# A four-layer attention and expert network: the last attention's maxima in four parts, its bodies 0.45 of a unit behind them

## The reference, cut to what matters

```python
def _L3_xattn_ref(x, cond, Wq, bq, Wkv, bkv, Wp, bp):
    q = (x @ Wq + bq).reshape(1, B * N, H, hd)          # 1024 queries, 16 heads of 16
    kv = (cond @ Wkv + bkv).reshape(1, -1, 2, H, hd)    # 1024 keys: all batches attend to all
    q = _fq_sym(q * scale, axis=-1)                     # rounded to 8 bits, one scale per token and head
    k = _fq_sym(k, axis=-1)
    v = _fq_sym(v, axis=2)
    attn = softmax(q @ k.T)
    attn = _fq_unsigned(attn, axis=-1)                  # round(attn / (max / 255)) * (max / 255)
    return (attn @ v).reshape(B, N, C) @ Wp + bp
x = x + tanh(g_xattn[3]) * _L3_xattn_ref(layernorm(x), ctx, ...)
x = x + tanh(g_ffn[3]) * _L3_ffn_ref(layernorm(x), ...)
```

## Time and profile before

| | us |
|---|---|
| median of 3 runs (1188.04 to 1189.3) | 1189.02 |
| the profiled execution's own time | 1187.16 |
| its span, first to last instruction | 1185.4 |
| TensorE busy in the span | 945.1 |
| VectorE busy | 660.6 |
| ScalarE busy | 438.3 |
| GpSimd busy | 383.5 |

### The profile page before, as it was taken

The page is one execution under the profiler, slowest core; times in us unless marked ns, Lnnn a source line. Parts: engine busy times, 40 slices in busy tenths (PEclk is TensorE's granted clock), DMA queues, the critical chain, the costliest instruction groups (busy, mean ns, idle before and its releaser), DMA issues.

```text
span 1185.4 us, 18900 instructions
## 1 busy us (share of the span) xinstructions
PE 945.1 (80%) x6620; PEld 558.2 (47%) x6620; DVE 660.6 (56%) x1574; ACT 438.3 (37%) x722; POOL 383.5 (32%) x515
## 2 busy tenths in 40 slices
PE   3899985798299999777379726999989997199993
PEld 1455544687044456554247612344434444156662
DVE  5678753462679334777623358787887852211111
ACT  1366662111056313443014300466546575021220
POOL 5233204332631003442050061356555565200002
PEclk9999996989589999996589956699999999599997
DMA  6434524684543004542327530101210002700002
GB/s 183 122 102 146 175 82 186 187 291 153 125 113 83 1 1 121 173 95 67 142 102 227 170 95 15 41 2 42 108 42 2 2 3 108 267 21 23 14 14 80
DMA packets 112700, 116.32 MB, mean 98 GB/s; under 512 B 58824, under 2 KB 102408, under 8 KB 109576
## 3 DMA queue, kind: packets, MB, share of 16 engines
q1 hardware_dynamic: 101760, 96.62, 26.5%
q10 hardware_dynamic: 7776, 10.10, 2.6%
q0 software_dynamic: 3072, 8.39, 2.3%
HBM read 88.17 MB, written 30.67 MB: 100 GB/s over the span
## 4 chain that ended last, share of the span: by engine, by line
PE 47%; DVE 14%; DMA 7%; issue 7%; POOL 6%; ACT 2%; SPq 1%; POOLq 0%; ACTq 0%; DVEq 0%
PE psT L1523 7%; PE psT L1223 5%; PE psT L1374 5%; PE psB L1338 4%; DVE mxp L1929 4%; PE psB L1223 4%; PE psO L1418 3%; PE psB L1537 3%; PE psT L1486 2%; PE psB L1588 2%; PE psO L1408 2%; DMA scr_k_high<-sk 1%; PE psO L1406 1%; POOL scr_sorted L2354 1%; PE psB L1564 1%
## 5 line engine op out<-in xcount | busy, mean ns | idle before, releaser
L1929 DVE TENSOR_REDUCE mxp<-psB 128x1 f32<-128x512 f32 x256 | 163.7, 684 | 37.5 <-PE psB L1338 36.7
L1374 PE MATMUL psT<-whole 99*128 99x256 bf16 (+2 forms) x1024 | 153.1, 275 | 10.0 <-issue 9.0
L1933 DVE TENSOR_REDUCE mxp<-psB 128x2 f32<-128x512 f32 x192 | 123.5, 684 | 31.6 <-PE psB L1344 31.2
L1675 ACT ACTIVATE Pt<-psT,ln 128x1024 f32<-128x1024 f32 x96 | 106.7, 1114 | 63.8 <-PE psT L1374 62.7
L1374 PEld LDWEIGHTS psT<-whole 99*128 99x128 bf16 (+2 forms) x1024 | 96.5, 102 | 54.1 <-issue 21.5
L1675 ACT ACTIVATE Pt<-psT 128x1024 f32<-128x1024 f32 x96 | 98.1, 1024 | 58.3 <-PE psT L1374 56.6
L1338 PE MATMUL psB<-whole 96*128 96x512 bf16 x256 | 96.2, 427 | 24.3 <-DMA whole<-scr_q 13.9
L2283 POOL TENSOR_TENSOR rstd<-vare,cst 128x1 f32<-128x1 f32 x64 | 35.8, 562 | 231.3 <-DVE vare L1836 231.0
L1344 PE MATMUL psB<-whole 96*128 96x256 bf16 x384 | 78.0, 306 | 36.0 <-DMA whole<-scr_q 20.3
L1523 PE MATMUL psT<-whole,qf 128*128 x176 | 82.3, 612 | 0.6 <-ACT qf L1729 0.6
L2342 POOL TENSOR_SCALAR nb_t<-Pt 128x1024 f16<-128x1024 f32 x64 | 67.2, 1051 | 39.5 <-ACT Pt L1675 37.4
(11 more groups left out here) (323 smaller groups left out, 1743.8 us busy)
## 6 DMA issues: line engine op xcount, KB each, us to landing
whole<-in_w SPq DMA_DIRECT2D x32, 512.0 KB, 5.2
whole<-in_w SPq DMA_DIRECT2D x5, 3072.0 KB, 10.3
xn<-scr_sorted ACTq DMA_DIRECT2D x42, 128.0 KB, 2.2
scr_q<-sq SPq DMA_DIRECT2D x48, 96.0 KB, 2.2
whole<-scr_q SPq DMA_DIRECT2D x24, 192.0 KB
whole<-scr_k SPq DMA_DIRECT2D x24, 192.0 KB, 3.5
scr_sorted_out<-xn SPq DMA_DIRECT2D x31, 128.0 KB, 2.4
scr_k<-sk SPq DMA_DIRECT2D x32, 96.0 KB, 1.9
```

Source lines behind the costliest of these rows:

```text
L1374: ins = pe.matmul(psT[:, s.n % 2, i * A.T:(i + 1) * A.T], lhsT=k_at[:, h * kw + s.c * P:h * kw + (s.c + 1) * P], rhs=q_at[:, h * A.T:(h + ...
L1675: act.activation(p_slot(A, s.p)[:, 0:4 * A.T], psT[:, s.n % 2, 0:4 * A.T], ACT.Exp, bias=bias, scale=scale).then_inc(T_used[s.n % 2], 1)
L1929: dve.tensor_reduce(mxp[:, s.un.g % 2, at:at + 1], psB[:, s.n % BANKS, :], AX.X, ALU.max).then_inc(bank_used[s.n % BANKS], 1)
L1933: dve.tensor_reduce(mxp[:, s.un.g % 2, at:at + 2], psB[:, s.n % BANKS, :].rearrange("p (h n) -> p h n", h=2), AX.X, ALU.max).then_inc(bank ...
```

## The change

The last attention has four parts in place of two (`parts=4`), so one part is 16 tiles of maxima and serves one group. Its times are set anew: maxima from `u + 1.0` to `u + 2.0`, each part's `negmax` 0.05 behind its end, the body at `u + 1.45`, the end at `u + 3.15`. The front of unit 1 is moved from `1 + t` to `1 + 0.17 + 0.6 t`. And the split of unit 0's queries is made on VectorE, where GpSimd only waits for it. The number of parts is now the unit's (`r.parts`), and the other attentions get new names for the same times: their order stays as it was.

```diff
+FIRST_PARTS = (1, 1, 1, 4)
+SECOND_FRONT = (0.17, 0.6)
...
-                           NC=chunks, has_max=has_max, G=heads // 4, halves=heads * d // P, parts=2 if layer == 3 else 1,
+                           NC=chunks, has_max=has_max, G=heads // 4, halves=heads * d // P, parts=4 if layer == 3 else 1,
...
-    dict(front=0, fronts=[...], rest=[...], store=0.42, packs=0.43, max=0.909, max_end=1.919, neg=1.973, body=1.639, end=3.415, start=0, span=1.008, max_first=1.026)]
+    dict(front=0, fronts=[...], rest=[...], store=0.42, packs=0.43, max=1.0, max_end=2.0, neg=2.05, body=1.45, end=3.15, start=0, span=1.0, max_first=1.0, first_end=2.0, first_body=1.45, first_neg=0.05, max_second=1.0)]
...
+            r.parts = FIRST_PARTS[A.layer] if u == 0 else A.parts
...
-            per = A.H * A.NC * P // 512 // A.parts
-            for part in range(A.parts):
+            per = A.H * A.NC * P // 512 // r.parts
+            for part in range(r.parts):
...
+                if A.layer == 3 and u == 1:
+                    times = [SECOND_FRONT[0] + SECOND_FRONT[1] * t for t in times]
...
-                begin = u + at["max"] if u else at["max_first"]
-                step = (u + at["max_end"] - begin) / A.parts
+                begin = at["max_first"] if u == 0 else 1 + at["max_second"] if u == 1 else u + at["max"]
+                end = at["first_end"] if u == 0 else u + at["max_end"]
+                step = (end - begin) / units[u].parts
+                later_by = at["neg"] - at["max_end"] if u else at["first_neg"]
...
-            streams += [(body(units[u]), u + at["body"], body_end), (finish(units[u]), body_end + at["start"], u + at["end"]),
+            streams += [(body(units[u]), u + at["body"] if u else at["first_body"], body_end), (finish(units[u]), body_end + at["start"], u + at["end"]),
...
-                elif s.kind == "split" and s.kind_of == "q" and s.un.u == 0:
+                elif s.kind == "split" and s.kind_of != "k1" and s.un.u == 0 and s.A.layer in (1, 3) and s.un.g is not None:
...
+                    else:
+                        evacuated(dve, u.m[0])
+                        evacuated(dve, u.m[1])
+                        src = qf[:, u.g % 2, :]
                     dve.wait_ge(parts_q, u.g)
                     dve.wait_ge(q_stored[u.g % 2], 32 * (u.g // 2))
-                    high, middle, low = [sq[:, u.g % 2, i, 0:256] for i in (2, 1, 0)]
-                    link(dve.tensor_copy(high, xn[:, 0, :]))
-                    link(dve.tensor_tensor(tmp[:, 0:256], xn[:, 0, :], high, ALU.subtract))
+                    high, middle, low = [sq[:, u.g % 2, i, 0:w] for i in (2, 1, 0)]
+                    link(dve.tensor_copy(high, src))
+                    link(dve.tensor_tensor(tmp[:, 0:w], src, high, ALU.subtract))
...
-                    if s.kind_of == "q" and u.u == 0:
+                    if u.u == 0 and u.g is not None and A.layer in (1, 3):
                         pool.wait_ge(parts_q, u.g + 1)
```

More of the change, by code:

```diff
@@ L69, in __init__ @@
         self.b0 = b0
-        self.k_packed = self.k_packed_before = None
+        self.k_packed = self.k_packed_before = self.parts = None
 P = 128
@@ L145 @@
 TIMES = [
-    dict(front=0.339, store=0.638, packs=0.793, max=1.019, max_end=1.817, neg=1.926, body=2.312, end=3.927, start=0.17, span=1.026, max_first=1.418),
-    dict(front=0.315, store=0.667, packs=1.608, max=1.871, max_end=2.713, neg=2.846, body=3.334, end=5.364, start=0, span=0.958, max_first=2.13),
-    dict(front=0.368, fronts=[-0.15, 0.1, 0.278, 0.262, 0.45], store=0.58, packs=0.684, body=1.604, end=3.227, start=0.084, span=1.053),
-    dict(front=0, fronts=[0.0, 0.005, 0.01, 0.02, 0.03, 0.04, 0.045, 0.045, 0.045, 0.045, 0.045, 0.058, 0.06, 0.079], rest=[0.0, 0.02, 0.06, 0.08, 0.11, 0.13, 0.15, 0.18, 0.21, 0.24, 0.27, 0.33, 0.34, 0.35], store=0.42, packs=0.43, max=0.909, max_end=1.919, neg=1.973, body=1.639, end=3.415, start=0, span=1.008, max_first=1.026)]
+    dict(front=0.339, store=0.638, packs=0.793, max=1.019, max_end=1.817, neg=1.926, body=2.312, end=3.927, start=0.17, span=1.026, max_first=1.418, first_end=1.817, first_body=2.312, first_neg=0.109, max_second=1.019),
+    dict(front=0.315, store=0.667, packs=1.608, max=1.871, max_end=2.713, neg=2.846, body=3.334, end=5.364, start=0, span=0.958, max_first=2.13, first_end=2.713, first_body=3.334, first_neg=0.133, max_second=1.871),
+    dict(front=0.368, fronts=[-0.15, 0.1, 0.278, 0.262, 0.45], store=0.58, packs=0.684, body=1.604, end=3.227, start=0.084, span=1.053, first_body=1.604),
+    dict(front=0, fronts=[0.0, 0.005, 0.01, 0.02, 0.03, 0.04, 0.045, 0.045, 0.045, 0.045, 0.045, 0.058, 0.06, 0.079], rest=[0.0, 0.02, 0.06, 0.08, 0.11, 0.13, 0.15, 0.18, 0.21, 0.24, 0.27, 0.33, 0.34, 0.35], store=0.42, packs=0.43, max=1.0, max_end=2.0, neg=2.05, body=1.45, end=3.15, start=0, span=1.0, max_first=1.0, first_end=2.0, first_body=1.45, first_neg=0.05, max_second=1.0)]
 def plan():
@@ L375, in st @@
                 s = add("st", A=A, un=r, g=g, c=c, first=(i == 0), n=take("T"), p=take("P"))
-                if A.has_max and c == 0 and g % (A.G // A.parts) == 0:
-                    s.neg = r.neg[g * A.parts // A.G]
+                if A.has_max and c == 0 and g % (A.G // r.parts) == 0:
+                    s.neg = r.neg[g * r.parts // A.G]
                 s.clip = take("clip") if A.layer == 2 else None
@@ L1178, in _ @@
                         r = A.rows + p3
-                        HP = A.H // A.parts
+                        HP = A.H // s.un.parts
                         sp.dma_start(QP[r:r + 1, s.un.g % 3, s.j * HP * A.T:(s.j + 1) * HP * A.T],
@@ L1351, in _ @@
                     pe.wait_ge(neg_split, s.i + 1)
-                    w = A.lows * A.H // A.parts
+                    w = A.lows * A.H // s.un.parts
                     for tc in range(A.TC):
```

21 lines of the change are left out of this document (11 added, 10 removed).

## The result

| | before | changed |
|---|---|---|
| median of the runs, us | 1188.53 (4 runs, 1183.26 to 1189.3) | 1210.41 (4 runs, 1208.53 to 1213.82) |
| span of the profiled execution | 1185.4 | 1208.9 |
| mean granted TensorE clock | 0.889 | 0.880 |
| VectorE busy | 660.6 | 669.9 |

The ratio is 1.0203, interval 1.0171 to 1.0235: the change costs about 22 us. (The kernel before has a fourth run here, 1183.26, which moved its median from 1189.02.) The forecast was 1188.0 within 1182.5 to 1193, so the result lies 22 us above it and far outside the range.

The account below looks back on a forecast made before the run. In the last attention VectorE and half-clock TensorE bound the maxima alone, TensorE the bodies beside maxima. Terms −10.6 + 3.2 + 1.8 + 1.2 + 2.0 + 1.4 = −1.0 us gave 1188.0 against 1189.02; range 1182.5 to 1193.

Parts of the forecast that it names:

- Steps 1 and 2: Ahead of the maxima: unit 0's split on VectorE (−1.6 us) and unit 1's `fn` behind 11 tiles (−0.6): −2.2.
- Step 3: Ahead of the first `st`: fifteen fewer maxima tiles, 30 in place of 45, at 0.609 us each: −9.1 us.
- a first `st` later than 742: Sign of a wrong forecast: the first `st`, expected near 739.6 us, coming after 742 would mean the start terms fail.
- Step 4: Beside the bodies: the fifteen maxima tiles moved there still cost TensorE 0.22 us each, +3.2 us.
- Step 5: Eight more sets of negative maxima: TensorE transposes +1.8 us; VectorE +1.2 for six sets, +2.0 for two among `quant` pieces.
- The half clock: Stretch of 1.2 GHz TensorE clock from the maxima into the first body: assumed to move along unchanged, no cost.
- rival B: Body ends of units 0 and 1: splits idle TensorE 3.5 us each and the clock falls; +3.5 us, 1192.5; chance 0.22.
- a clock below 1.00 in several windows after 760: Sign of a wrong forecast: granted TensorE clock under 1.00 after 760 us would point to costly splits at body ends.
- Step 6: Body ends of units 0 and 1: GpSimd splits of units 2 and 3 idle TensorE; +1.4 us, between −1 and +4.
- Rival A: Last attention: small waits vanish in each other, only TensorE's extra work comes back; −5.6 us, 1183.4; chance 0.25.
- C: Clock rises at another time: early −5.5 us (1183.5), chance 0.05; late +3.5 us (1192.5), chance 0.04.

Follow-up runs that it names:

- e1: Kernel before (two parts, old order) with only unit 0's split moved to VectorE; ratio to before 0.9996, body 246.6 us.
- e9: The changed kernel with the front of units 2 and 3 moved 0.13 of a unit earlier; ratio to before 1.006, body 261.6 us.
- e2: e1 with four parts in place of two, at the old distance; ratio to before 1.0147, body 264.1 us.
- e12: e2 with one VectorE operation per set of negative maxima in place of five, middle and low parts zero; ratio to before 0.996, body 248.1 us.
- e17: The changed kernel with four operations of each negative-maxima set on GpSimd, one on VectorE, `negmax` 0.03 unit later; ratio to before 1.0021, body 259.7 us.
- e18: e1 with four operations of each negative-maxima set on GpSimd, one on VectorE, `negmax` 0.03 unit later; ratio to before 0.9956, body 242.5 us.
- e16: e9 with four operations of each negative-maxima set on GpSimd, one on VectorE, `negmax` 0.03 unit later; ratio to before 0.9962, body 249.0 us.
- e14: e1 with the split of units 2 and 3 just ahead of the body's last `round`, `store` and `packs` behind it; ratio to before 1.0023, body 248.5 us.
- e13: The changed kernel with the splits of units 2 and 3 behind the body's last `round`; ratio to before 1.0122, body 265.4 us.
- e3: The changed kernel with the quantising pieces of units 2 and 3 ahead of the next `negsplit`; ratio to before 1.0189, body 271.0 us.
- e15: e9 with one VectorE operation per set of negative maxima in place of five, middle and low parts zero; ratio to before 0.9882, body 241.5 us.

## Why the prediction failed, step by step

*Steps 1 and 2, start of the maxima, −2.2.* Right: −1.9 (15.8 to 13.9 us), of which the split alone 1.5 (e1).

*Step 3, first `st`.* Right in kind: first reduction to first `st` is 6.9 us shorter, forecast −9.1 + 0.7 = −8.4. The sign "a first `st` later than 742" is met (746.2), but only because this execution came to the attention 4.7 us later, its order up to there being unchanged.

*Step 4 and the transposes of step 5, +3.2 + 1.8 = +5.0 of TensorE's work.* Right to a few us: +2.6 in the change, +5.0 in e9, and for the transposes +1.2 (e2) to +1.9 (e12).

*Step 5, VectorE's part of the sets, +1.2 + 2.0 = +3.2.* **This step failed.** It set 1.4 us of VectorE against 11.2 us of idle time a unit and charged 0.2. Measured, the eight added sets cost about 12 us by VectorE's time alone: 16.0 (e2 to e12) or 15.9 (the change to e17) for all sixteen, less 4.1 for the eight old ones (e1 to e18). With the places mended it is 8.5 (12.6 from e9 to e16, less 4.1). That is 1.1 to 1.5 us a set, nearly as long as a set takes: 1.26 us in the change, and 1.57 in e2, where its operations wait longer for GpSimd's rounds. Of the 16.0, 9.1 are idle time and 7.6 clock (and work 0.7 the other way), and step 5 has no term for the clock. The account that fits, worked out and not tested by itself: the room that counts is that of a slot. Two reductions are 2 × 0.685 = 1.37 us of the 1.63 that a slot takes, so 0.26 is left, and there are three PSUM banks; a lump of 1.4 us is worked off only over five slots.

*The half clock, "I let this stretch of half clock move along unchanged".* Right for the stretch that reaches from the start into the body (it ended 9 us behind the first `st` before and also after), but the sum has no term for new stretches. **This is the second failure**, +14.8 us. No pause of TensorE longer than 1.83 us came ahead of the first fall, and half clock went on although TensorE was then busy 6.00 of 6 (818 to 824). The sign that the prediction gave for B, a clock below 1.00 in several windows after 760, was met.

*Step 6 and rival B, the split.* The stalls were sized well: 2.9 and 3.2 us in the change, 3.1 in e14. The sum left out the clock behind them. B had it, at 3.5 us of half clock for each split, but added 1.75 us once where its own premise gives 3.5 for the two; with that it would have stood at +5.2 and not +3.5. e14's half clock, 10.2 us in two stretches against 3.4 in e1, is a loss of 3.4 and bears B out. In the change 8.8 us of clock loss hung on the place (e13): there the stall comes close behind the `negsplit` in the quantising stretch, and each was priced as if it stood alone.

*Rival A* fell: the waits didn't vanish in each other. *C* wasn't it either: the first rise came as before.

*Two slips in the sums, which decide nothing.* The worse end of the range adds up to +5.5 (−10.6 + 3.2 + 3.7 + 2.4 + 2.8 + 4) and not +5.9, and fifteen tiles at 0.22 are 3.3.

**The account.** The bodies of e1 and of before are equal (246.6 and 246.7), and between the change and e1 the runs make a chain. Going over e17: the sets off VectorE 15.9 (e17), the two places 10.7 (e16), two parts and far bodies 6.5 (e18), the eight old sets' VectorE time back −4.1 (e1): together 29.0. Going over e9: the places 14.0 (e9), the sets off VectorE 12.6 (e16), then 6.5 and −4.1 as before: 29.0 again. So of +28.9 us of body the added sets' VectorE time is 8.5 to 12, the places 10.7 to 14, as one or the other is taken first, and four parts and near bodies by themselves 6.5, of which 4.8 is TensorE's work. Each link is the difference of two single profiles. The ratios, whose intervals are 2 to 6 us to either side, give for the whole time 21.6 from the change to e17 and 7.0 on to e16, or 16.9 from the change to e9 and 11.6 on to e16: the same two causes, each known to a few us only. Start −6.9, and −1.9 ahead of it: together +20.1, to compare with the 21.9 between the medians.

Not settled: how the 10 to 14 us of the places divide in time (by the bodies e3 wins 5, e13 10, both 14, and by the ratio e3 wins nothing clear); why e15's body is 6.6 us under e12's although more maxima lie beside it; and what e16 would be with its negative maxima in time.
